# A recurrent two-layer kernel: gate/up pair 1 of the next tile at the end of a round, small products regrouped, decay-row masks later

## What is computed

```python
# layer 0: s is an RWKV6 mixer, 4 heads of 64
a = tanh(xxx @ time_maa_w1)            # five mixing ranks w, k, v, r, g
xw, xk, xv, xr, xg = x + xx * (maa + a @ time_maa_w2)
w = time_decay + tanh(xw @ time_decay_w1) @ time_decay_w2
y = wkv6(xr @ W_r.T, xk @ W_k.T, xv @ W_v.T, w, u)   # recurrent state per head
s = (groupnorm(y) * gamma + beta) * silu(xg @ W_g.T) @ W_o.T
# layer 0: ffn with the 2 largest of every 4 hidden values kept
h = sparsify_2to4(silu(x @ w_gate) * (x @ w_up));  ffn = h @ w_down
# layer 1: s is a state-space mixer of 8 heads (X, B, C, step dt per head), gated by silu(res)
# layer 1: ffn = (silu(x @ w_gate.T) * (x @ w_up.T)) @ w_down.T, hidden width 1024
```

## Time and profile before

| | |
|---|---|
| runs | 739.51, 742.24, 743.68 us; median 742.24 |
| the profiled execution | 740.68 us, span 738.9 us |
| granted clock, mean over the span | 0.998 |
| busy | PE 715.5 us (97%), DVE 496.8 (67%), ACT 343.4 (46%), POOL 77.5 (10%) |
| chain that ended last | PE 90% of the span, DVE 5% |

### The profile page before, as it was taken

How to read it: one execution, slowest core, us unless ns; L and a number is a source line. 1 busy time by engine, 2 the same in 40 slices (tenths; PEclk the granted TensorE clock), 3 DMA queues, 4 the chain that set the end, 5 groups by cost and what they waited for, 6 DMA issues and landing times.

```text
span 738.9 us, 17998 instructions
## 1 busy us (share of the span) xinstructions
PE 715.5 (97%) x6896; PEld 588.5 (80%) x6896; DVE 496.8 (67%) x1207; ACT 343.4 (46%) x678; POOL 77.5 (10%) x85
## 2 busy tenths in 40 slices
PE   5988999999999999999999999999999999999998
PEld 3766788878888788887888868888788878888777
DVE  5975689537895468845787558964689536895132
ACT  1422684236821567115862168512683236821680
POOL 6301101101011011100111001110101101011020
PEclk9999999999999999999999999999999999999999
DMA  7900450136301353013521154102530135301350
GB/s 250 392 19 28 132 87 3 15 87 145 59 2 25 107 115 59 5 40 94 121 48 16 29 145 87 31 15 72 148 70 2 15 86 145 59 2 28 117 114 16
DMA packets 122444, 55.93 MB, mean 76 GB/s; under 512 B 104384, under 2 KB 114176, under 8 KB 120832
## 3 DMA queue, kind: packets, MB, share of 16 engines
q1 hardware_dynamic: 122368, 54.76, 30.0%
HBM read 42.35 MB, written 12.40 MB: 74 GB/s over the span
## 4 chain that ended last, share of the span: by engine, by line
PE 90%; DVE 5%; issue 2%; ACT 1%; DMA 0%; POOL 0%; DVEq 0%; ACTq 0%; SPq 0%; POOLq 0%
PE psum L1487 69%; PE psum L1590 3%; PE psum L1702 2%; PE psum L1717 2%; PE psum L1515 1%; PE psum L1560 1%; PE psum L1728 1%; PE psum L1926 1%; DVE gate L1262 1%; PE psum L1755 1%; PE psum L1623 1%; PE psum L1549 1%; PE psum L1868 1%; PE psum L1572 1%; PE psum L1663 1%
## 5 line engine op out<-in xcount | busy, mean ns | idle before, releaser
L602 ACT ACTIVATE BC<-psum 64x256 f32<-64x256 f32 x128 | 81.5, 637 | 3.0 <-PE psum L1487 1.3
L1487 PE MATMUL psum<-xn1T,sb_n_gate 128*128 128x256 f32 x256 | 62.2, 386 | 0.0
L1487 PE MATMUL psum<-xn1T,sb_n_up 128*128 128x256 f32 x256 | 60.5, 379 | 0.0
L1487 PE MATMUL psum<-xnT,sb_f_gate 128*128 128x256 f32 x240 | 58.5, 386 | 0.0
L1487 PE MATMUL psum<-xnT,sb_f_up 128*128 128x256 f32 x240 | 57.6, 382 | 0.0
L1487 PEld LDWEIGHTS psum<-xn1T,sb_n_up 128*128 128x128 f32 x256 | 48.6, 190 | 6.6
L1487 PEld LDWEIGHTS psum<-xn1T,sb_n_gate 128*128 128x128 f32 x256 | 46.8, 190 | 8.8 <-DVE gate L1312 2.7
L1487 PE MATMUL psum<-sb_f_down,hid 128*128 128x256 f32 x224 | 50.2, 382 | 0.0
L1487 PEld LDWEIGHTS psum<-xnT,sb_f_up 128*128 128x128 f32 x240 | 44.8, 190 | 6.4 <-issue 0.3
L1487 PEld LDWEIGHTS psum<-xnT,sb_f_gate 128*128 128x128 f32 x240 | 44.2, 189 | 6.8 <-issue 0.2
L1487 PE MATMUL psum<-sb_n_down,hidB 128*128 128x256 f32 x224 | 49.5, 379 | 0.0
(11 more groups left out here) (257 smaller groups left out, 1483.3 us busy)
## 6 DMA issues: line engine op xcount, KB each, us to landing
cs_row<-cs_dram SPq DMA_DIRECT2D x8, 1024.0 KB, 4.9
x_dram<-gate SPq DMA_DIRECT2D x8, 512.0 KB, 2.8
cs_half<-cs_dram SPq DMA_DIRECT2D x16, 256.0 KB, 5.7
hidB<-x_dram SPq DMA_DIRECT2D x8, 512.0 KB, 5.6
b_dram<-B_turned SPq DMA_DIRECT2D x32, 128.0 KB, 3.3
hidB<-b_dram SPq DMA_DIRECT2D x8, 512.0 KB, 4.2
X<-in_x SPq DMA_DIRECT2D x9, 256.0 KB, 3.3
XT<-in_x_turned SPq DMA_DIRECT2D x8, 256.0 KB, 3.6
```

Source lines behind the costliest of these rows:

```text
L602: ins = a_.activation(cols[:, par, 2 * pair:2 * pair + 2, :], src[64 * par:64 * par + 64, :, s, :], ACT.Identity)
L1487: ins = t_.matmul(ps(t, name)[first_row:first_row + rows, col:col + n], w, x, start=(k == 0), stop=(k == len(ws) - 1))
```

## The change

1. p1 of the next tile is made at the end of a round, behind pair 0, on PE. ACT makes the silu of both pairs there (`next_gates`), and p1 is now "whole" except in the first tile. The six unread products of the first round go.
2. In the middle of a full round p1 is gone; C0 and C1 come before `first_levels`, so that D stands next to L; the two `scores` stand together, before `chunk_states`; `within` stands before `outputs`.
3. Layer 1's pairs n2 and n3 are split: gate n2 before F0, up n2 and gate n3 before s0.
4. DVE: both `hidden_p` at the head of a round, first half's comparisons in one piece before the gate mix, the transposes of B before `end_args`, `gated_1` before the second half's comparisons, among others.
5. POOL masks the decay rows of a full round only when DVE has finished level 3 (`lev_ready` of 4).
6. First round: the down product's first half in four parts around `keys_turned`, `chunk_states` and `outputs`. Last round: n3 before `states`.
7. The bank tables follow: k moves to bank 2, p1g to bank 7 and p1u to bank 4; sc0, st, n0u, n2u, F1 move to bank 4, sc1, ys1, n1u, n3u to bank 6.

```diff
-FILLS = [["mix_w", "dw", "w0", "k", "mix_g0", "L0", "M0", "k0T", "p3g", "F0"],
-         ["p0g", "mix_k", "w1", "p1g", "mix_g1", "L1", "M1", "kv", "p3u", "yT"],
-         ["p0u", "mix_r", "p1u", "r", "D0", "g", "p2g", "Y0", "s0"],
+FILLS = [["mix_w", "dw", "w0", "mix_g0", "L0", "M0", "k0T", "p3g", "F0"],
+         ["p0g", "mix_k", "w1", "mix_g1", "L1", "M1", "kv", "p3u", "yT"],
+         ["p0u", "mix_r", "k", "r", "D0", "g", "p2g", "Y0", "s0"],
          ["a", "mix_v", "v", "D1", "p2u", "Y1"],
-         ["csum", "C1", "sc1", "ys1", "n1u", "n3u"],
+         ["csum", "C1", "sc0", "st", "n0u", "n2u", "F1", "p1u"],
          ["dt", "B0", "res0", "sc3", "n0g", "n2g", "s1"],
-         ["X0", "B1", "res1", "sc0", "st", "n0u", "n2u", "F1"],
-         ["X1", "C0", "sc2", "ys0", "n1g", "n3g"]]
+         ["X0", "B1", "res1", "sc1", "ys1", "n1u", "n3u"],
+         ["X1", "C0", "sc2", "ys0", "n1g", "n3g", "p1g"]]
...
@@ POOL
+                    if a:
+                        pool.wait_ge(lev_ready, a.count(6, 4))
+                        pool.sem_inc(passed, 1)
                     g.affine_select(out=cs_row[:, :, :], in_=cs_row[:, :, :], compare_op=ALU.is_ge, fill=NEG, base=0,
@@ ACT
+                def next_gates():
+                    for n in range(2):
+                        ffn_tanh(a.next(), f"p{n}", th[n], None)
+                    exp_tables()
...
                 if a and b:
-                    ffn_tanh(a, "p0", th[0], th_ready)
-                    exp_tables()
...
-                    ffn_tanh(a, "p1", th[1], th_ready)
+                    ffn_abs(a, 1)
...
                     ffn_tanh_1()
+                    if a.reg is not None:
+                        next_gates()
@@ DVE, full round
                     hidden_p(a, 0)
+                    hidden_p(a, 1)
...
                     decay_sums(a)
-                    hidden_p(a, 1)
+                    compare(0)
                     mix_g_scaled(a)
...
                     own_taken(a)
-                    end_args()
                     B_by_block(0)
                     B_by_block(1)
+                    end_args()
...
                     gate_0()
-                    sparse_compare(a, 0, 0)
                     high_taken(a)
...
-                    sparse_compare(a, 0, 1)
-                    sparse_compare(a, 0, 2)
-                    states_0()
                     B_decayed()
                     decayed_scores(0)
+                    states_0()
+                    for n in (2, 1, 3):
+                        decayed_scores(n)
                     hidden_p(a, 2)
...
+                    gated_1()
                     compare(1)
-                    gated_1()
@@ PE, full round
                     carries()
-                    project_p(a, 1, "u")
-                    project_p(a, 1, "g")
...
                     ssd_proj(b, "B1", "w_B", 1)
-                    first_levels()
                     ssd_proj(b, "C0", "w_C", 0)
                     ssd_proj(b, "C1", "w_C", 1)
+                    first_levels()
                     low_levels(a)
...
                     scores(0)
+                    scores(1)
                     chunk_states()
                     project_p(a, 3, "g")
                     project_p(a, 3, "u")
-                    scores(1)
                     states()
+                    within()
                     outputs()
-                    within()
                     across()
                     ffn_n(b, 0)
                     ffn_n(b, 1)
+                    gate_n(b, 2)
                     down_0()
                     out_turned()
-                    ffn_n(b, 2)
+                    up_n(b, 2)
+                    gate_n(b, 3)
                     out_0()
-                    ffn_n(b, 3)
+                    up_n(b, 3)
                     out_1()
                     ffn_1(b, hidB)
                     if a.reg is not None:
                         next_gate_0()
                         next_up_0()
+                        ffn_p(a.next(), 1)
@@ PE, first round
-                    keys_turned()
-                    chunk_states()
...
-                    down_part(a, 0, 0, 4)
+                    down_part(a, 0, 0, 2)
+                    keys_turned()
+                    down_part(a, 0, 2, 4)
+                    chunk_states()
+                    down_part(a, 1, 0, 2)
                     outputs()
-                    down_part(a, 1, 0, 4)
+                    down_part(a, 1, 2, 4)
...
                     next_up_0()
-                    kept_at_work("xT1", 6)
+                    ffn_p(a.next(), 1)
                     turned_1()
@@ PE, last round
                     ffn_n(b, 2)
+                    ffn_n(b, 3)
                     states()
-                    ffn_n(b, 3)
                     within()
```

35 lines of the change are left out of this document (21 added, 14 removed).

## The result

The changed kernel takes **746.48 us** (median of 9 runs, 745.31 to 748.81), the kernel before beside it 742.06 (739.51 to 743.68). The ratio is 1.0063 with a 95% interval of 1.0048 to 1.0078: slower, and outside the range of 722 to 737. The profiled execution took 745.55 us, its span is 743.7.

A forecast was written before the change was run, and what follows sets the result against it. PE's products were taken to bound the 88.54 us round. Seven full rounds at 1.3 give 9.1, the first two rounds 5.9, the last nothing: 15.0 us off, so 727.2 us on the median, range 722 to 737.

The forecast's parts named there:

- The stretch D, C, L: PE from B1 to g: 8.62 us becomes 8.10 in the new order, 0.52 gained per full round.
- the middle without cover: Rival: without p1 between decays and r, PE waits for DVE's levels each full round; up to 751.4 us; chance 0.04.
- the rival that has it fall near 54 us: Rival: the clock falls elsewhere in the first round; gain 11.7, time 730.5 us; chance 0.14.
- The 1.8: First round's down product in parts keeps the clock up: 1.8 us gained, bounds 0 and 2.1.
- The mask: POOL's decay-row mask, moved later: costed at 0; as rival it holds DVE, 733.0 to 741.3 us, chance 0.10.
- Per full round 1.3: Sum per full round: 0.52 + 0.33 + 0.26 + 0.2 + 0.2 - 0.2 = 1.3 us; seven rounds give 9.1.
- The scores: Score products on PE: 0.33 us from no longer using the gate's bank, 0.26 from standing together, per full round.
- The changes of array shape: Within before the outputs: fewer array shape changes follow one another; 0.2 us gained per round, bounds 0 and 0.4.
- The weight loads and n2 before F0: Earlier gated_1 shortens the weight-load wait of n1's gate; gate n2 precedes F0: 0.2 us per round, bounds 0 and 0.39.
- What becomes tight: Before g, a 0.1 us wait for bank D0 and a 0.1 late weight load: 0.2 lost per full round.
- The edges: First two rounds gain 3.4 + 0.7 + 1.8 = 5.9 us; the last round nothing, within 0.6 either way.
- The pair's 3.46: p1 moved to a round's end: first round grows by 0.1, second is 3.46 us shorter; together 3.4 gained.

The follow-up runs named there:

- e5: Changed kernel with 64 spare semaphore instructions on PE, dealt out behind the large products ahead of D in the middle section's rounds; 749.52 us.
- e6: Changed kernel with 128 spare semaphore instructions on PE, dealt out behind the large products ahead of D in the middle section's rounds; 788.67 us.
- e7: Changed kernel with 256 spare semaphore instructions on PE, dealt out behind the large products ahead of D in the middle section's rounds; 946.29 us.
- e9: Changed kernel with 128 spare semaphore instructions at the very start of PE's program, none in any round; 743.10 us.
- e13: Changed kernel with 32 small identity products (128 instructions) on PE ahead of the first transposes; 729.64 us.
- e8: Kernel before with one part of the change alone: C0 and C1 ahead of D, so D stands directly before L; 740.53 us.
- e15: Changed kernel with 24 small identity products (96 instructions) on PE ahead of the first transposes; 725.71 us.
- e2: Kernel before with only the wait for level 3 put in front of POOL's mask; 743.53 us.
- e14: Kernel before with 32 small identity products on PE ahead of the first transposes; 744.49 us.
- e17: Kernel before with 24 small identity products on PE ahead of the first transposes; 740.33 us.
- e16: e13 without the later mask: POOL masks the decay rows from about when they have landed; 746.81 us.
- e3: Changed kernel with C0 and C1 put back between D and L, the mask staying late; 734.47 us.
- e18: Changed kernel with the load of X's rows sent out behind the load of B's rows; 743.26 us.
- e11: Changed kernel with 60 spare semaphore instructions at the start of PE's program; 744.93 us.
- e10: Changed kernel with C0 between D and L and C1 between the second and third low level of L; 739.65 us.

## Why the prediction was wrong, and where it was right

**The step that failed: "The stretch D, C, L".** I gave L its 2.00 us wherever it stands and the whole stretch from B1 to g 8.10. It took 277.46 - 267.56 = 9.90. Of the 1.80 too many 1.68 are the hole. Shown: it hangs on where the loop's instructions lie (e5, e6, e7, e9, e13) and not on the order of the products as such (e8), it ends behind the landing of one block of instructions, and it is gone where no block is fetched (e15): a wait of PE for its own instructions. Where the border does no harm (e15) the stretch takes 268.83 - 260.42 = 8.41, and 0.33 of it is the wait for D0's bank: 8.08 beside the 8.10. All of the forecast's working was on what the products need; none on how they are delivered. Nor did I have a rival for it: each of mine had another engine, the clock or a bank in it. The nearest in effect, the middle without cover, came to 2.1 us a round as the point from which it decides; the hole and its slow parts cost 1.7 to 3.8.

**The clock** was expected to fall in the first round or not at all. In the changed kernel it stayed at 1.00 there, from 46 to 60 us, as forecast, and fell behind the holes of later rounds. But the rival that has it fall near 54 us came true in the profiled executions of e13 and e15: at 0.50 for 3.4 us from 57.5 and 55.4, behind a wait of 1.87 that the changed kernel has too. PE in e15:

```profile
55.24 4.54 PE L1554 MATMUL psum<-sb_f_down,hid 128*128 128x256 f32 x12 [1.87 <-DVE hid L1124]
```

The same twelve records take 2.86 in the changed kernel, so the slow part costs 1.7. And the one in the earlier trace rows, which the forecast set out to save, is missing in e2, e14 and e17, whose first rounds do the work of the kernel before. The 1.8 was read from one execution of something that comes and goes.

**The mask**, costed at 0: its place is worth 17.2 us once the hole is gone (e13 against e16). My reason was that DVE waits 1.09 behind it anyway. That slack belongs to the order in which p1 stands ahead of r. With p1 gone, r and the levels come 3.4 earlier in the round, and an early mask meets the level chain instead of the last mix addition. In its new place it costs nothing, as said: DVE's copies of its own products keep their 0.77 beside it. I had that step right for what the change does and wrong for what it saves. The Trainium skill ("SBUF — State Buffer", Who interferes with whom), whose second half no row showed then, is borne out: the copies read PSUM and one mask tile and were not held, the level product with two SBUF inputs went from 0.42 to 2.02.

**Per full round 1.3.** e15 against e17: 88.53 - 86.99 = 1.54. The starts of the groups in their timelines (rounds from 248.05 in e17 and from 244.17 in e15) take the terms apart:

| stretch on PE | before, e17 | changed, e15 | gain | forecast |
|---|---|---|---|---|
| head to B1 (p1 leaves) | 19.71 | 16.25 | 3.46 | 3.46 |
| B1 to g | 8.62 | 8.41 | 0.21 | 0.52 - 0.2 |
| g to k0T | 10.03 | 10.01 | 0.02 | 0 |
| behind k0T: scores and kv | 3.73 | 3.13 | 0.60 | 0.33 + 0.26 |
| p3, states, within, Y, across | 9.21 | 8.91 | 0.30 | 0.2 |
| n0 to the next head (p1 comes) | 37.23 | 40.27 | -3.04 | -3.46 + 0.2 |

The scores came out as said. The changes of array shape gave 0.3 where I took 0.2; by the rule of "TensorEngine Tiling" in the Trainium skill it would have been 0.4, and 0.3 lies between the two. The weight loads and n2 before F0 gave 0.42, the upper bound and not the middle. "What becomes tight" was mis-sized the other way: 0.33 for D0's bank (2.4 us in seven rounds) where I had a wait of 0.1. The errors went both ways, and the sum came out 0.24 better than said.

**The edges** came out worse. In the changed kernel the second round starts at 68.91, where 68.4 was forecast. That alone settles little, as the same first round took 57.2 us in e3 and 60.3 in e18. Against the forecast stand the profiles of e17 and e15: first round 58.29 and 58.39, with the slow part of 1.7 in e15 alone, where -1.7 was forecast; second round 89.49 and 87.06, that is 1.54 and 0.9 for ACT's copy wait (0.7 on record), which is gone. The pair's 3.46 I put into the second round, but that is a round of the loop, and it gains a pair at its end as it loses one in the middle. The pair that goes is that of the round of tile 7, which I had at zero: 85.09 and 81.64 up to the last round's first product. There 1.54 + 3.46 should be gained and 3.45 is: the last round's load is late by 0.8, as forecast, and some 0.6 goes in small delays behind the third pair that the loop's rounds do not have. The last round itself is longer by 0.5 where I had no change: its wait before the states, 1.3 in the earlier trace rows, is 0.45 in e17, and in e15 n3's up product waits 0.9 for the decayed scores, a wait that I had as 0.5 at `across`.

**The time** of the hole-free kernel, 725.71, lies 1.5 under the 727.2 on record, and the change is worth 14.6 where 15.0 were forecast. Part of that is luck: seven full rounds gave 7 x 1.54 = 10.8 us in place of 9.1, so the edges gave 3.8 in place of 5.9. The main mechanism of the rounds was right, and the kernel was slower by a thing that the order only uncovered.

## What to carry to other kernels

A hole on an engine that ends with "issue", at the same record in every round and in products that wait for nothing, is a question of instruction supply: look whether a packet of the instruction queue lies in or just before it. Test it by a shift ahead of the loop, since that changes no round. Try two or three sizes, as a shift can move the border from the run of small products to just behind the loop's head. A change that shortens an idle stretch also takes away the slack that made another collision harmless, so price a move of POOL's work in the new order, not in the old.

## What the runs showed of the hardware that was not expected

- A block of 16 KB is fetched by one packet; that it holds 256 instructions, as the Trainium skill ("Runtime: NRT & Kernel Launch", Instruction fetch mechanics) has it, agrees with e7, where 256 more bring the hole back to the same record. In the round shown PE runs dry at 275.53, the packet begins between 274.80 and 274.95, and work resumes at 277.21. The holes were 1.68 to 2.22 us in the changed kernel and up to 2.2 in e7. For small products this is not "mostly hidden", as the Trainium skill's section has it: D and L up to the hole, 152 matmul records beside their weight loads, took 2.7 us.
- A loop can stay in PE's instruction memory: 21 fetches in place of 66 in e15 and e17. The Trainium skill (the same page and section) gives PE 128 KiB, 2048 instructions, and says that "there's no instruction cache that benefits from spatial locality". The body has 859 matmuls and 859 weight loads on record in the changed kernel's round from 340.26, and instructions without a record beside them; it is not shown how many. That it fits in e15 and not in e13, 32 instructions on, agrees with a limit near that figure; that the loop ran from 130 to 580 us without a fetch contradicts the sentence on the cache.
- What a loop without fetches is worth by itself: 0.1 to 0.4 a round between e15 and e9. In the kernel before the rounds stay as they were (88.53 against 88.54 to 88.62), so that the 2 us of e17 are not explained by it.
- A semaphore instruction at the start of PE's program took about 153 ns: the first product came at 21.80 us with 128 of them and at 11.39 with 60. The 114 ns by which e11 was planned left out that they begin well before the 7.2 us are over. Behind large products one cost about 65 ns in e6 (95.7 - 87.3 a round, for 128).
- The clock fell to 1.2 GHz for a few microseconds after PE had stood 1.7 to 2.2 us in three rounds of the changed kernel, and not in the other rounds with holes of 1.7 to 2.0. In e13 and e15 it fell behind a wait of 1.87 in the first round, and not behind the same wait in the changed kernel. What tells them apart stays open.
- Also open: what makes the fetch late at these borders, since in e18 it began 1.8 us and more after the last transfer, and why C1 inside L (e10) was worse than e3.
